# Two mixture-of-experts layers: one-hots by narrow comparisons, gathers issued one tile earlier, weights loaded between stores

## The chip, the cores and the metric

One core of a Trainium2 chip runs the whole network in one launch. The metric is the device time of that launch in microseconds (us). Three runs of the kernel before gave 2677.88, 2682.55 and 2683.99 us, so the median is 2682.55 us. "us" is always microseconds and "ns" nanoseconds.

## The reference, cut to what matters

The network has eight stages on x of shape (8, 512, 256), that is 4096 tokens of 256 numbers: attention, mixture, attention, a feed-forward layer, a windowed attention, mixture, attention, a feed-forward layer. Each stage is `x = x + stage(layernorm(x))`. The change touches only the two mixtures, called L0 and L2 here:

```
z = layernorm(x)
logits = z @ gate                       # 8 experts
take the two largest, weights = softmax over the two
L0 expert e:  h = z @ w1[e] + b1[e]     # 256 -> 512
              h = gelu(layernorm(h) * g[e] + b[e])
              y = h @ w2[e] + b2[e]     # 512 -> 256
              out = layernorm(sum of weight * y, plus z) * ln_g + ln_b
L2 expert e:  h = gelu(z @ w1[e] + b1[e])   # 256 -> 1024
              y = h @ w2[e] + b2[e]         # 1024 -> 256
              out = sum of weight * y
x = x + out
```

## The kernel before, in words

x stays in the on-chip memory, 128 tokens to a tile, 32 tiles of 256 columns, in 8 batches of 4 tiles. Everything is float32 unless said otherwise. A mixture has three parts that follow one another, with a barrier between them.

**Dispatch** (`dispatch`, lines 793 to 1051) finds which expert each token goes to. ScalarE normalises a batch (`normalise`, line 917), SyncE stores it to the rows_in table in device memory (line 856), and TensorE turns it (line 873) and multiplies it by the gate (line 881). In L0 there is a buffer for each of the 8 batches. In L2 there are two, so `normalise(b)` waits until the store of batch b - 2 has landed. After the first store SyncE issues `k.late(sp)` and the expert constants. In L2 `k.late` issues eight loads of 1 MB, one expert's first layer each, all in a row, and the stores of the other seven batches come behind them on the same queue. In L0 `k.late` does nothing, since those weights came earlier.

VectorE then picks the two experts of each token (`select`, lines 965 to 976, once for each half of the tokens) and works out each row's place in a table of 71 tiles of 128 rows, each owned by one expert. To turn places into lists of row numbers it goes through 8 chunks of 8 columns (lines 1030 to 1036). A chunk needs two sets of 0/1 vectors in bf16: `at_tile`, 8 x 71, made by one VectorE comparison (line 1033), and `at_slot`, 8 x 128, made by another (line 1035: 1024 float32 elements against a broadcast column). `at_tile` is multiplied by two kinds of constants, by ScalarE (line 938) and by GpSimd (line 947), and TensorE multiplies the result by `at_slot` (line 904). The end of this is `src` and `dst`, 71 columns of row numbers, and `owner`, the expert of each tile.

**Experts** (L0: `experts`, lines 1082 to 1263; L2: `experts_gelu`). The 71 tiles run one after the other. In L0, step j of each engine is:

- TensorE: transpose h of tile j (line 1154), first layer of tile j + 2 (line 1145), transpose the rows of tile j + 3 (`turn`, line 1136), second layer of tile j (line 1164).
- ScalarE: gelu of tile j (line 1187), then the copy of the transposed rows of tile j + 3 (line 1179).
- VectorE: add b1 to tile j + 2 and take its mean and variance (lines 1207 to 1213), then add b2 to the output of tile j (line 1227), then centre h of tile j + 2 (line 1217).
- GpSimd: send the output of tile j - 1 to the rows_out table (`send_rows`, line 1277, an indirect DMA that waits for line 1227), fetch the rows of tile j + 3 (`fetch_rows`, line 1269, an indirect DMA that waits until the buffer's former rows are transposed), take the inverse root of the variance of tile j + 2 (line 1242), and in each odd step up to 31 add the bias `ln_b` to two tiles of x (`bias`, line 1246).

Gathered rows have two buffers, used in turn. An engine runs its own list in order, so a wait also holds whatever comes behind it. TensorE, ScalarE and VectorE read the owner of a tile into a register in each step (`value_load`).

**Combine** (L0: `combine_norm`) reads the rows back, weighs, adds and normalises them. It is not changed.

Of the kernel before, what the change touches and what calls it, by code (L numbers as in the profile page):

```python
# [16 lines left out]
BF16 = mybir.dt.bfloat16  # L17
# [776 lines left out]
def dispatch(nc, k, L):  # L794
# [12 lines left out]
    with ctx:  # L807
        gate = sb(nm + "gate", [P, DC, E])
        shift = sb(nm + "shift", [P, NT])
        Z = NB if L == 0 else 2  # L810
# [19 lines left out]
        code = sb(nm + "code", [P, NT])  # L830
        top = [sb(f"{nm}top{j}", [P, NT]) for j in range(TOPK)]
# [18 lines left out]
        with nc.Block() as block:  # L850
            @block.sync
            def _(sp):
                sp.dma_start(gate[:, :, :], k.a[f"L{L}_gate"]).then_inc(w_in, 16)
                for b in range(NB):
                    sp.wait_ge(z_done, b + 1)
                    sp.dma_start(k.zs[P + b * SEQ:P + (b + 1) * SEQ, :].rearrange("(t p) d -> p t d", p=P),
                                 z[b % Z].rearrange("p (t d) -> p t d", t=TPB)).then_inc(stored[b % 2], 16)
                    if b == 0:
                        k.late(sp)
                        load_expert_constants(sp, k, L)  # L860
                for s in range(2):
                    sp.wait_ge(stored[s], 16 * NB // 2)
                sp.wait_ge(k.zeroed, 16)
# [77 lines left out]
            @block.gpsimd  # L941
            def _(pool):
                for c in range(CHUNKS):
                    s = c % 2
                    pool.wait_ge(hot_done, c + 1)
                    hi = k.cst[:, C_HI + c * NJ:C_HI + (c + 1) * NJ, None].to_broadcast([P, NJ, NTILES])
                    pool.tensor_tensor(names[s][:, :, 0, :], at_tile[s][:, :, :], hi, ALU.mult).then_inc(hi_done, 1)

            @block.vector
            def _(dve):  # L950
# [29 lines left out]
                dve.sem_inc(centred, 1)  # L980
                for h in range(2):
# [48 lines left out]
                for c in range(CHUNKS):  # L1030
# [4 lines left out]
                    dve.tensor_tensor(at_slot[s][:, :, :], k.cst[:, None, C_I:C_I + P].to_broadcast([P, NJ, P]),  # L1035
                                      slot[:, own, None].to_broadcast([P, NJ, P]), ALU.is_equal).then_inc(slot_done, 1)
# [45 lines left out]
def experts(nc, k, L):  # L1082
# [15 lines left out]
    with ctx:  # L1098
        w1, w2 = k.w1, k.w2
        b2, bt, b1, gt, post_b = k.expert_constants  # L1100
        if norm:
            st = [sb(f"{nm}st{s}", [P, 6]) for s in range(2)]
# [21 lines left out]
        with nc.Block() as block:  # L1124
# [114 lines left out]
            def _(pool):  # L1239
# [4 lines left out]
                def bias(i):  # L1244
                    xs = k.x[:, i * (2 * D):(i + 1) * (2 * D)].rearrange("p (t d) -> p t d", t=2)
                    pool.tensor_tensor(xs, xs, post_b[:, None, :].to_broadcast([P, 2, D]), ALU.add)
# [289 lines left out]
def load_expert_constants(eng, k, L):  # L1536
    for t, (name, spread) in zip(k.expert_constants, (("b2", True), ("bt", False), ("b1", True), ("gt", False),
                                                      ("ln_b", True))[:5 if L == 0 else 2]):
# [5 lines left out]
def mixture(nc, k, L):  # L1544

    ctx, sb, ps, sem = scoped(k)
    with ctx:
# [4 lines left out]
            [sb("x0_b1", [P, E * F]), sb("x0_gt", [P, E * FC]), sb("x0_post_b", [P, D])] if L == 0 else [None] * 3)  # L1552
# [806 lines left out]
def build(nc, a, out, stages="a0 m0 a1 f1 w2 m2 a3 f3"):  # L2359
    nothing = lambda sp: None  # L2360
    with ExitStack() as ctx:
# [35 lines left out]
        if "m0" in todo:  # L2397
            k.w1, k.w2 = room("m0_w1", E * DC * F0), room("m0_w2", E * F0 // P * D)
            k.w_count = 16 * 2 * E
            k.late = m0_weights if first_stage("m0") else nothing  # L2400
# [28 lines left out]
        if "m2" in todo:  # L2429
            k.w1 = room("m2_w1", E * DC * F2)  # L2430

            def m2_late(eng):
                if "a1" not in todo:
                    load_second_layers(eng, k, 2)
                load_first_layers(eng, k, 2, range(E))
# [67 lines left out]
```

## Time and profile before

| | |
|---|---|
| median of three runs | 2682.55 us |
| the profiled execution, whole | 2691.29 us |
| its span | 2689.5 us |
| TensorE busy (matmul) | 2075.9 us, 77% |
| TensorE busy (weight load, overlapping) | 1525.3 us, 57% |
| VectorE busy | 1327.2 us, 49% |
| ScalarE busy | 936.7 us, 35% |
| GpSimd busy | 598.0 us, 22% |
| mean granted TensorE clock | 0.877 of full |

The span is one execution from its first to its last instruction. The profile names engines PE (TensorE matmul), PEld (TensorE weight load), DVE (VectorE), ACT (ScalarE), POOL (GpSimd) and SP (SyncE, SPq for what its queue issues). The page's own split of the span into 40 slices shows L0's mixture in slices 4 to 15 and L2's in slices 25 to 34. The busy share is a mean over stages with different limits, so each stage has to be read by itself.

### The profile page before, as it was taken

The numbers are of one execution on the slowest core, as the hardware profiler recorded it, in microseconds if no ns is written. First come the engines' busy times: TensorE is split into PE (matmuls) and PEld (weight loads), VectorE is DVE, ScalarE is ACT, GpSimd is POOL, SyncE is SP. The second block draws the span as 40 slices with busy tenths as digits, with TensorE's granted clock in tenths as the row PEclk, the third lists the DMA queues.
The fourth block names the chain that finished last, engine by engine and source line by source line (L and its number), as shares of the span: only waits on it lengthen the run. The fifth ranks groups of instructions, "written<-read, shape, count | busy, mean of one in ns | idle before, by whom it ended". The sixth has DMA issues, their size and how long they took to land. (4 is left out here: it accounts for less than half of the span.)

```text
span 2689.5 us, 37832 instructions
## 1 busy us (share of the span) xinstructions
PE 2075.9 (77%) x11915; PEld 1525.3 (57%) x11931; DVE 1327.2 (49%) x2988; ACT 936.7 (35%) x2034; POOL 598.0 (22%) x580
## 2 busy tenths in 40 slices
PE   6997466666666611997999795579999999699687
PEld 4666243443443310665566663579999999366355
DVE  5873522222222257676777562422222222588787
ACT  3444221112112132443333122323333333355487
POOL 1210433332222255012011000122222222122000
PEclk9996688888878865998999896579999999799799
DMA  6003100000000032200000003111111111410000
GB/s 227 1 1 113 36 29 29 27 27 27 29 28 28 27 119 78 105 1 1 12 0 0 6 10 145 59 44 38 36 35 37 37 35 32 137 48 1 1 32 32
DMA packets 66898, 115.34 MB, mean 43 GB/s; under 512 B 13520, under 2 KB 50512, under 8 KB 63728
## 3 DMA queue, kind: packets, MB, share of 16 engines
q1 hardware_dynamic: 51536, 74.56, 8.0%
q0 software_dynamic: 13680, 37.37, 4.4%
q10 hardware_dynamic: 1584, 2.13, 0.3%
q8 instruction: 58, 0.95, 0.2%
q14 instruction: 40, 0.33, 0.0%
HBM read 82.71 MB, written 31.33 MB: 42 GB/s over the span
## 5 line engine op out<-in xcount | busy, mean ns | idle before, releaser
L1336 PEld LDWEIGHTS psum<-e_xT,e_w 128*128 128x128 f32 x2272 | 269.7, 195 | 8.4 <-ACT e_xT L1366 4.9
L1336 PE MATMUL psum<-e_xT,e_w 128*128 128x128 f32 x2272 | 270.3, 278 | 4.2 <-ACT e_xT L1366 4.2
L1373 ACT ACTIVATE e_hT<-psum,x_bt 128x128 f32<-128x128 f32 x568 | 154.6, 383 | 337.3 <-PE psum L1336 323.4
L268 POOL TENSOR_TENSOR rstd<-lnt,half 128x4 f32<-128x4 f32 (+1 forms) x72 | 81.0, 1126 | 820.0 <-DVE lnt L262 820.0
L1345 PE MATMUL psum<-m_w,e_hT 128*128 x1136 | 256.8, 379 | 0.0
L1164 PE MATMUL psum<-m_w,e_hT 128*128 x568 | 215.9, 547 | 39.7 <-issue 36.1
L1345 PEld LDWEIGHTS psum<-m_w,e_hT 128*128 128x128 f32 x1136 | 210.4, 190 | 25.7
L1277 POOL DMA_INDIRECT rows_out<-e_y,dst x106 | 111.1, 1048 | 512.0 <-DVE e_y L1227 337.0
L1394 DVE COPY e_w<-m_w 128x2048 f32 x71 | 87.1, 1227 | 239.0 <-PE psum L1336 228.5
L1227 DVE TENSOR_TENSOR e_y<-psum,x_b 128x256 f32<-128x256 f32 x71 | 30.2, 425 | 353.2 <-PE psum L1164 352.6
L1187 ACT ACTIVATE e_hT<-psum,x_bt,x_gt 128x128 f32<-128x128 f32 x284 | 107.0, 457 | 275.2 <-PE psum L1154 275.2
L1164 PEld LDWEIGHTS psum<-m_w,e_hT 128*128 128x128 f32 x568 | 146.4, 269 | 85.0 <-issue 57.5
L1136 PE MATMUL psum<-cst,e_x 128*128 128x128 f32 x142 | 32.8, 315 | 197.9 <-DMA e_x<-rows_in,src 197.9
L696 DVE TENSOR_REDUCE a_mx<-psum 128x8 f32<-128x512 f32 x192 | 123.2, 684 | 106.8 <-PE psum L500 106.5
L1136 PEld LDWEIGHTS psum<-cst,e_x 128*128 128x128 f32 x142 | 15.1, 147 | 256.1 <-DMA e_x<-rows_in,src 245.9
L1269 POOL DMA_INDIRECT e_x<-rows_in,src x142 | 139.2, 980 | 63.5 <-issue 42.0
L625 ACT ACTIVATE a_pT<-psum 128x512 f32<-128x512 f32 x192 | 104.0, 593 | 126.8 <-PE psum L550 126.8
L1145 PE MATMUL psum<-m_w,e_xT 128*128 x284 | 144.4, 633 | 1.4 <-ACT e_xT L1179 1.2
L1806 PE MATMUL psum<-f_w,f_q 128*128 128x256 f32 x512 | 123.9, 388 | 14.7 <-DVE f_q L1693 14.7
L481 PE MATMUL psum<-a_cx,att_wk 128*128 128x64 f32 x192 | 29.9, 305 | 130.4 <-DMA a_cx<-in_ctxT 130.4
L1806 PEld LDWEIGHTS psum<-f_w,f_q 128*128 128x128 f32 x512 | 98.9, 194 | 55.5 <-issue 30.5
L699 DVE TENSOR_TENSOR a_pr<-psum,a_mx 128x512 f32<-128x512 f32 x192 | 122.9, 682 | 0.7
(285 smaller groups left out, 3935.0 us busy)
## 6 DMA issues: line engine op xcount, KB each, us to landing
m_w<-in_L_ffn_w SPq DMA_DIRECT2D x16, 1024.0 KB, 15.2
m_w<-in_L_ffn_w SPq DMA_DIRECT2D x16, 512.0 KB, 12.2
c_g<-rows_out SPq DMA_DIRECT2D x16, 512.0 KB, 5.0
a_ar_g<-rows_out SPq DMA_DIRECT2D x16, 512.0 KB, 5.1
x_res<-in_x SPq DMA_DIRECT2D x8, 512.0 KB, 7.1
rows_in<-x_z SPq DMA_DIRECT2D x8, 512.0 KB, 7.4
rows_in<-r_work SPq DMA_DIRECT2D x8, 512.0 KB, 3.3
out_x<-x_res SPq DMA_DIRECT2D x8, 512.0 KB, 2.9
```

Of the source, the lines that this page charges most:

```text
L625: act.activation(pT[t // 2][:, g * SLOTS:(g + 1) * SLOTS, t % 2, :], tr_b[g][:, :, :], ACT.Exp).then_inc(t_evac, 1)
L696: dve.tensor_reduce(mx[g][:, :], wide[g], AX.X, ALU.max).then_inc(s_max, 1)
L699: dve.tensor_tensor(pr[t % 2][:, g * W:(g + 1) * W].rearrange("p (h l) -> p h l", h=HPC), wide[g], mx[g][:, :, None].to_broadcast([P, HPC, ...
L1145: mm = pe.matmul(h_b[s][:, c * 512:(c + 1) * 512], xT[s][:, kk, :], w1[:, bass.ds(e * (DC * F) + (kk * F + c * 512), 512)], start=(kk == 0 ...
L1164: mm = pe.matmul(y_b[:, 0:D], hT[s][:, f, :], w2[:, bass.ds(e * (FC * D) + f * D, D)], start=(f == 0), stop=(f == FC - 1))
L1187: g = act.activation(hT[s][:, f, :], hT_b[:, f, :], ACT.Gelu, bias=bt[:, col], scale=gt[:, col] if norm else 1.0)
L1269: pool.indirect_dma_start(out=xin[j % 2][:, :], out_offset=None, in_=k.zs[:, :], in_offset=bass.IndirectOffsetOnAxis(ap=k.src[:, j:j + 1], ...
L1277: pool.indirect_dma_start(out=k.ys[:, :], out_offset=bass.IndirectOffsetOnAxis(ap=k.dst[:, j:j + 1], axis=0), in_=y[j % 2][:, :], in_offse ...
L1336: mm = pe.matmul(h_b[s][:, f, :], w1[:, kk, f * P:(f + 1) * P], xT[s][:, kk, :], start=(kk == 0), stop=(kk == DC - 1))
L1345: mm = pe.matmul(y_b[s][:, 0:D], hT[s][:, f, :], k.w2[:, bass.ds(e * (FC * D) + f * D, D)], start=(f == 0), stop=(f == FC - 1))
L1373: g = act.activation(hT[s][:, f, :], h_b[s][:, f, :], ACT.Gelu, bias=bt[:, bass.ds(e * FC + f, 1)])
L1806: mm = pe.matmul(yb[t % 2][:, 0:D], q[s][:, g, t * P:(t + 1) * P], w2[:, g, :], start=(g == 0), stop=(g == FC - 1))
```

## The change

1. In the dispatch of both mixtures `at_slot` is made by 8 VectorE comparisons of 128 bf16 elements with one float32 column each (`tensor_scalar`), in place of one comparison of 1024 float32 elements with a broadcast. There are 64 of them in a dispatch in place of 8. The numbers 0 to 127 are copied once to bf16 (`numbers`).
2. In the experts of L0, GpSimd fetches the rows of tile j + 4 ahead of sending tile j - 1, in place of tile j + 3 behind it. One more fetch is issued before the loop.
3. The bias `ln_b` of L0 is added to x by GpSimd in the dispatch, in 8 additions of 1024 columns, each when its batch has been normalised, and no longer in the experts, where it took 16 of 512 columns. It has its own buffer and semaphore now, and its load is issued ahead of the stores.
4. In the dispatch of L2 the expert constants are issued after the first store as before, but the eight loads of 1 MB are spread: one behind each of the stores 1 to 6, two behind store 7.

```diff
@@ dispatch, tiles
+        if L == 0:
+            post_b, post_in = sb(nm + "post_b", [P, D]), sem(nm + "post_in")
+        numbers = sb(nm + "numbers", [P, P], BF16)
@@ dispatch, SyncE
                 sp.dma_start(gate[:, :, :], k.a[f"L{L}_gate"]).then_inc(w_in, 16)
+                if L == 0:
+                    sp.dma_start(post_b[:, :], k.a["L0_ffn_ln_b"].partition_broadcast(P)).then_inc(post_in, 16)
                 for b in range(NB):
                     sp.wait_ge(z_done, b + 1)
                     sp.dma_start(k.zs[P + b * SEQ:P + (b + 1) * SEQ, :].rearrange("(t p) d -> p t d", p=P),
                                  z[b % Z].rearrange("p (t d) -> p t d", t=TPB)).then_inc(stored[b % 2], 16)
                     if b == 0:
-                        k.late(sp)
                         load_expert_constants(sp, k, L)
+                    k.late(sp, b)
@@ dispatch, GpSimd
+                if L == 0:
+                    pool.wait_ge(post_in, 16)
+                    for b in range(NB):
+                        pool.wait_ge(z_done, b + 1)
+                        xs = k.x[:, b * (TPB * D):(b + 1) * (TPB * D)].rearrange("p (t d) -> p t d", t=TPB)
+                        pool.tensor_tensor(xs, xs, post_b[:, None, :].to_broadcast([P, TPB, D]), ALU.add)
@@ dispatch, VectorE
+                then(dve.tensor_copy(numbers[:, :], k.cst[:, C_I:C_I + P]))
...
-                    dve.tensor_tensor(at_slot[s][:, :, :], k.cst[:, None, C_I:C_I + P].to_broadcast([P, NJ, P]),
-                                      slot[:, own, None].to_broadcast([P, NJ, P]), ALU.is_equal).then_inc(slot_done, 1)
+                    for i in range(NJ):
+                        nj = c * NJ + i
+                        o = dve.tensor_scalar(at_slot[s][:, i, :], numbers[:, :], slot[:, nj:nj + 1], None, ALU.is_equal)
+                    o.then_inc(slot_done, 1)
@@ experts, GpSimd (A is 2 in L0)
                 for j in range(A + 1):
                     fetch_rows(pool, k, j, xin, xT_ps)
-                pool.wait_ge(k.const_in, k.consts)
                 for j in range(A):
                     root(j)
+                fetch_rows(pool, k, A + 1, xin, xT_ps)
                 for j in range(NTILES):
+                    if j + A + 2 < NTILES:
+                        fetch_rows(pool, k, j + A + 2, xin, xT_ps)
                     if j > 0:
                         send_rows(pool, k, j - 1, y, y_done)
-                    if j + A + 1 < NTILES:
-                        fetch_rows(pool, k, j + A + 1, xin, xT_ps)
                     if j + A < NTILES:
                         root(j + A)
-                    if j % 2 and j // 2 < NT // 2:
-                        bias(j // 2)
@@ the loads of L2
-            def m2_late(eng):
+            def m2_late(eng, b):
...
-                load_first_layers(eng, k, 2, range(E))
+                if b > 0:
+                    load_first_layers(eng, k, 2, (b - 1,))
+                if b == NB - 1:
+                    load_first_layers(eng, k, 2, range(b, E))
```

## Rows read from the trace of the kernel before

**Rows 1.** Engine busy times by window: PE, PEld, DVE, ACT, POOL, clock, DMA, GB/s
```profile
600.00:700.00 100.00, 62.27 (x199) 39.01 (x198) 28.63 (x67) 20.79 (x55) 29.64 (x34) 0.88 0.09 28
1860.00:1960.00 100.00, 100.00 (x689) 94.22 (x689) 23.13 (x28) 34.33 (x126) 26.49 (x27) 1.00 0.11 35
...
1660.00:1686.00 26.00, 4.82 (x38) 4.72 (x38) 0.00 (x0) 2.28 (x5) 0.00 (x0) 0.57 0.96 383
```

**Rows 2.** Waits in L0's experts (298 to 962 us): total, times, longest
```profile
PE psum L1136 <- DMA e_x<-rows_in,src: 197.9, 69, 8.3
```

**Rows 3.** Timeline of one step of L0's experts: start, length, engine, line, operation
```profile
502.68 0.42 DVE L1227 TENSOR_TENSOR e_y<-psum,x_b 128x256 f32<-128x256 f32 x1 [5.63 <-PE psum L1164]
...
503.40 1.08 POOL L1277 DMA_INDIRECT rows_out<-e_y,dst  x1 [5.70 <-DVE e_y L1227]
...
504.78 0.97 POOL L1269 DMA_INDIRECT e_x<-rows_in,src  x1 [0.30 <-issue]
...
507.55 0.44 PE L1136 MATMUL psum<-cst,e_x 128*128 128x128 f32 x2 [2.68 <-DMA e_x<-rows_in,src]
```

**Rows 4.** Line 1227, all its instructions: ns min/median/max, first and last start
```profile
L1227 DVE TENSOR_TENSOR e_y<-psum,x_b x71: 424/425/426, 321.6 to 958.1; 128x256 f32<-128x256 f32 x71
```

**Rows 5.** Timeline of TensorE alone, a warm step, then the prologue
```profile
603.40 1.99 PE L1164 MATMUL psum<-m_w,e_hT 128*128 x8 [0.55 <-issue]
605.23 0.60 PE L1154 MATMUL psum<-cst,e_h 128*128 128x128 f32 x4
605.66 1.90 PE L1145 MATMUL psum<-m_w,e_xT 128*128 x4
...
309.11 1.98 PE L1145 MATMUL psum<-m_w,e_xT 128*128 x4 [0.56 <-ACT e_xT L1179]
...
310.92 0.38 PE L1136 MATMUL psum<-cst,e_x 128*128 128x128 f32 x2
```

**Rows 6.** Timeline of L0's last steps, where no rows are gathered
```profile
940.86 3.77 PE L1164 MATMUL psum<-m_w,e_hT 128*128 x8 [0.30 <-issue]
...
947.97 0.69 DVE L1207 TENSOR_TENSOR e_h<-psum,x_b 128x512 f32<-128x512 f32 x1 [2.21 <-PE psum L1145]
...
950.53 0.42 DVE L1227 TENSOR_TENSOR e_y<-psum,x_b 128x256 f32<-128x256 f32 x1 [0.69 <-issue]
950.87 0.54 DVE L1217 TENSOR_SCALAR e_h<-e_h,e_mv,e_rs 128x512 f32<-128x512 f32 x1
...
953.61 0.60 PE L1154 MATMUL psum<-cst,e_h 128*128 128x128 f32 x4
...
956.00 1.99 PE L1164 MATMUL psum<-m_w,e_hT 128*128 x8 [1.80 <-ACT e_hT L1187]
```

**Rows 7.** Timeline of L2's dispatch, then of L0's: ScalarE
```profile
1685.77 2.07 ACT L917 ACTIVATE r_work<-x_res,r_shift,rstd 128x256 f32<-128x256 f32 x4 [23.72 <-DMA rows_in<-r_work]
...
235.01 1.02 ACT L924 ACTIVATE r_work<-psum 128x1024 f32<-128x1024 f32 x1 [2.03 <-PE psum L873]
```

**Rows 8.** Timeline of a chunk of L0's dispatch
```profile
272.39 1.22 DVE L1035 TENSOR_TENSOR att_wq<-cst,r_slot 128x1024 bf16<-128x1024 f32 x1
...
272.55 2.05 POOL L947 TENSOR_TENSOR r_work<-r_work,cst 128x568 bf16<-128x568 bf16 x1 [56.90 <-DVE r_work L1033]
273.52 1.68 DVE L1033 TENSOR_TENSOR r_work<-cst,r_tile 128x568 bf16<-128x568 f32 x1
...
275.12 1.21 DVE L1035 TENSOR_TENSOR att_wk<-cst,r_slot 128x1024 bf16<-128x1024 f32 x1
```

**Rows 9.** Timeline: small VectorE operations with a scalar
```profile
205.22 0.16 DVE L259 TENSOR_SCALAR mean<-mean 128x4 f32<-128x4 f32 x1
205.29 0.16 DVE L260 TENSOR_SCALAR lnt<-lnt 128x4 f32<-128x4 f32 x1
...
267.45 0.20 DVE L1010 TENSOR_SCALAR r_turn<-r_rank 128x64 f32<-128x64 f32 x1
```

**Rows 10.** Groups of instructions of the whole run: GpSimd
```profile
L436 POOL TENSOR_TENSOR x_res<-x_res,att_bo 128x1024 f32<-128x1024 f32 x24 | 56.8, 2365 | 8.6 <-ACT a_z L589 8.6
```

More of the change, by code:

```diff
@@ L1099, in experts @@
         w1, w2 = k.w1, k.w2
-        b2, bt, b1, gt, post_b = k.expert_constants
+        b2, bt = k.expert_constants[0:2]
         if norm:
+            b1, gt = k.expert_constants[2:4]
             st = [sb(f"{nm}st{s}", [P, 6]) for s in range(2)]
@@ L1242, in root @@
                     pool.tensor_tensor(rs[j % 2][:, :], ve[j % 2][:, :], k.half[:, 0:1], ALU.pow).then_inc(rsq, 1)
-                def bias(i):
-                    xs = k.x[:, i * (2 * D):(i + 1) * (2 * D)].rearrange("p (t d) -> p t d", t=2)
-                    pool.tensor_tensor(xs, xs, post_b[:, None, :].to_broadcast([P, 2, D]), ALU.add)
                 for j in range(A + 1):
                     fetch_rows(pool, k, j, xin, xT_ps)
-                pool.wait_ge(k.const_in, k.consts)
                 for j in range(A):
                     root(j)
+                fetch_rows(pool, k, A + 1, xin, xT_ps)
                 for j in range(NTILES):
+                    if j + A + 2 < NTILES:
+                        fetch_rows(pool, k, j + A + 2, xin, xT_ps)
                     if j > 0:
                         send_rows(pool, k, j - 1, y, y_done)
-                    if j + A + 1 < NTILES:
-                        fetch_rows(pool, k, j + A + 1, xin, xT_ps)
                     if j + A < NTILES:
                         root(j + A)
-                    if j % 2 and j // 2 < NT // 2:
-                        bias(j // 2)
                 send_rows(pool, k, NTILES - 1, y, y_done)
@@ L1536, in load_expert_constants @@
 def load_expert_constants(eng, k, L):
-    for t, (name, spread) in zip(k.expert_constants, (("b2", True), ("bt", False), ("b1", True), ("gt", False),
-                                                      ("ln_b", True))[:5 if L == 0 else 2]):
+    for t, (name, spread) in zip(k.expert_constants, (("b2", True), ("bt", False), ("b1", True), ("gt", False)
+                                                      )[:4 if L == 0 else 2]):
         src = k.a[f"L{L}_ffn_{name}"]
@@ L1551, in mixture @@
         k.expert_constants = [sb(f"x{L}_b2", [P, E * D]), sb(f"x{L}_bt", [P, E * FC])] + (
-            [sb("x0_b1", [P, E * F]), sb("x0_gt", [P, E * FC]), sb("x0_post_b", [P, D])] if L == 0 else [None] * 3)
+            [sb("x0_b1", [P, E * F]), sb("x0_gt", [P, E * FC])] if L == 0 else [])
         if L == 0:
@@ L2399, in build @@
             k.w_count = 16 * 2 * E
-            k.late = m0_weights if first_stage("m0") else nothing
+            k.late = (lambda eng, b: m0_weights(eng) if b == 0 else None) if first_stage("m0") else lambda eng, b: None
         if "a0" in todo:
@@ L2430, in build @@
             k.w1 = room("m2_w1", E * DC * F2)
-            def m2_late(eng):
-                if "a1" not in todo:
+            def m2_late(eng, b):
+                if b == 0 and "a1" not in todo:
                     load_second_layers(eng, k, 2)
-                load_first_layers(eng, k, 2, range(E))
+                if b > 0:
+                    load_first_layers(eng, k, 2, (b - 1,))
+                if b == NB - 1:
+                    load_first_layers(eng, k, 2, range(b, E))
             k.late = m2_late
```

## The prediction

> **What bounds the kernel now.** I read the busy times by window first, then the waits of the stage that stands out, then its timeline step by step, and at the end the two dispatches side by side.
>
> The windows show two expert stages that look alike in code and not in time [rows 1]. In L2's experts TensorE is busy 100.00 us of 100, at full clock. In L0's it is busy 62.27 us of 100 and no other engine passes 30, so nothing is saturated there: something late is waited for. The waits name it [rows 2]: TensorE's transpose (L1136) sits idle 197.9 us in 69 waits for gathered rows, 2.9 us a tile.
>
> The timeline shows why the rows are late [rows 3]. The output of a tile starts at 502.68; GpSimd sends it from 503.40 on; only then, at 504.78, does it issue the gather, because in its list the gather stands behind the send; the rows are used at 507.55. The second layer comes behind that transpose in TensorE's list, so the next output waits for it, and so the next send and the next gather. Output, send, gather, transpose, second layer is a closed loop, 4.87 us of it (502.68 to 507.55) outside TensorE. Line 1227 runs 71 times from 321.6 to 958.1 [rows 4]: 70 steps in 636.5 us, 9.09 us each.
>
> The dispatches have one clear stall [rows 7]: ScalarE waits 23.72 us in L2 for a store of the second batch that stands behind eight 1 MB loads. L0 runs the same code with more buffers and without those loads.
>
> **Part 1, gathers a tile further ahead (the large term).** GpSimd now issues gather j + 4 before it waits for output j - 1. The gather waits for its buffer alone, which is free once rows j + 2 are transposed, a step and more before. From issue to use it takes 2.77 us (504.78 to 507.55) [rows 3] and it now has nearly two steps. So the loop is cut and the wait of [rows 2] goes. What is queued behind the gather's wait on GpSimd is send j - 1 and root j + 2; the transpose waited for stands ahead of the second layer that the send waits for, so this wait is over first. GpSimd's own work in a step is the gather 0.97, the send 1.08, a root and gaps: under 4 us.
>
> What is late next? TensorE itself. A warm step is the second layer 1.83 us (start to start, 603.40 to 605.23), the transposes of h 0.43 (605.23 to 605.66), the first layer 1.81 (309.11 to 310.92) and the transpose of rows 0.38 [rows 5]: 4.45 us. Two other chains must stay below it:
> - gelu: from the transposes of h to the second layer that waits for gelu it takes 2.39 us (953.61 to 956.00) [rows 6], and 1.83 for the second layer follow: 4.22 us.
> - VectorE: 2.56 us from L1207 to L1227 (947.97 to 950.53), 0.34 to L1217, 0.54 for it, and at most 0.69 to the next [rows 6]: 4.13 us.
>
> Both are below 4.45 but close, so there is no further slack. The step could be as short as 4.22 (the transposes overlap more than their length says). It could be 5.00, if the 0.55 us between the transpose of rows and the second layer stays [rows 5]. That gap is a register load behind a wait; with the wait gone TensorE's sequencer can run ahead and hide it. I take 4.45, clock at full level (2.4 GHz): L2's experts hold 1.00 at 100% busy, where L0's have 0.88 with holes in them [rows 1].
>
> 70 steps x (9.09 - 4.45) = **325 us** saved. Bounds: 70 x (9.09 - 4.22) = 341, and 70 x (9.09 - 5.00) = 286.
>
> **Part 2, loads between the stores of L2.** The 23.72 us stall goes [rows 7]. What takes its place: each store now stands behind at most one load of 1 MB (the second store behind the 1 MB of constants). At 383 GB/s [rows 1] a load is 2.7 us and a store of 0.5 MB 1.4, together 4.1 a batch. A batch of L0 takes ScalarE 1.02 + 2.07 us of work and 2.03 of waiting for TensorE [rows 7], 5.1 in all, so the queue just keeps up. With two buffers I allow 2 us for the first batches: **22 us** saved. Bounds 17 (a us lost in each later batch) and 24. Two loads are left behind the last store, 5.5 us at that rate, while the eight chunks alone last four times as long; the experts find them landed. SyncE has nothing else to do there.
>
> **Part 3, the bias moved.** 8 additions of 2.37 us [rows 10], 19 us on GpSimd, which had been idle 56.90 us when the first chunk came [rows 8]; they follow the batches. They end long before the chunks, whose products are the next thing in GpSimd's list. They can hold up `select` of the first half of the tokens, which is early anyway. In the experts GpSimd was waiting, not working, so taking the bias out saves nothing there. Its 128 KB load ahead of the first store costs under 1 us, and L0's stores have buffers of their own. If the cover were gone in full it would cost 19 us. I take **0**.
>
> **Part 4, narrow comparisons.** The wide comparison holds VectorE 1.13 us (272.39 to 273.52) [rows 8]. A chunk takes 2.73 us (272.39 to 275.12), and the three operations lie end to end: GpSimd's product spans 2.05 but the comparison at 273.52 ends, at 275.20, 0.60 us after the product's end at 274.60, where its own elements at about 1 ns each need 0.59. I read this as turns: VectorE's comparison, GpSimd's product (about 1 us of its 2.05), VectorE's next. So a chunk changes by what VectorE's part changes by. The trace has no 128-column bf16 comparison with a column. Nearest rows [rows 9]: two tiny scalar operations start 0.07 us apart (205.22, 205.29), and one of 64 float32 columns is 0.20 long with its pipeline. I take 0.10 each, nearer the start-to-start figure, since no wait stands between the eight: 0.80 against 1.13, 0.33 x 16 chunks = **5 us** saved. Ends: at 0.20 each a loss of 0.47 x 16 = 7.5 us; at 0.07 a gain of 9, and 15 more if GpSimd's product no longer takes its turn. The copy of the numbers to bf16 falls where VectorE waits for logits: 0.
>
> One rule speaks against this part. The Trainium skill, "VectorE: DVE Perf Modes", in the section on the TRN2 errata, says that the memory latency is paid between instructions, so one large operation pays it once and many small ones each time, and advises 512 elements or more. Its cycle formula there (58 plus the elements over 4, at 0.96 GHz) would give, as an estimate, 94 ns for each of the eight, 0.75 us together; its section "The DRAIN you can't avoid" says that the next operation can't issue until the pipeline is empty. By the first the sum would be as mine within 1 us; by the second it would be near the losing end. The 0.07 us between two starts speaks against the second [rows 9].
>
> **The sum.** Own time 2691.3 - 325 - 22 - 0 - 5 = 2339 us. The profiled execution is 8.7 us above the median of the three runs, so against the median: **2331 us**, 13% less.
>
> **The rivals.**
> - The comparisons are held one behind the other, 0.20 us each with the whole length paid: +7.5 in place of -5, 2343 us. For it: the small operations last 0.16 to 0.20. Against: their starts lie closer. It moves the sum, not the verdict. Chance 0.20.
> - The register loads stay in TensorE's (or VectorE's) step: 5.00 us a step, 39 us more, 2370 us. For it: 0.55 us of idle is there even in warm steps [rows 5], and 0.69 us before L1227 where its input was ready [rows 6]. Against: in both places a wait had just held the sequencer. Chance 0.13.
> - TensorE stays at its lower level (1.2 GHz) in L0's experts: the second layer lasts 3.77 us there against 1.99 [rows 5, 6]; a step of 2 x 4.45 = 8.9 us saves 13, giving 2642 us. For it: the clock is below full today. Against: L2's experts [rows 1]. Chance 0.05.
> - The change does not do what it says: the gather still lands late (held in GpSimd's list by something I took as early), and the gains of the dispatch are eaten by port conflicts with the moved bias. About 2683 us. Against: each wait ahead of the gather belongs to the step before. Chance 0.02.
> - Slower: denser matmuls bring the granted clock down, and it stays down after L0's experts. The place is L2's experts, about 520 us at full clock with TensorE always busy; at the lower level they last 520 us more. With all other gains as above it decides from two thirds of that stage (350 of 520); in full, 2850 us. For it: only that the clock varies today. Against: in L2's experts it is 1.00 through hundreds of us at 100% busy [rows 1]. Chance 0.03.
>
> **How the numbers follow.** The likeliest case has 0.57, and its own range is 2305 to 2355 (step 4.22 to 4.7). Low end of the whole range: 2683 - 341 - 24 - 18 = 2300. High end: the 5.00 us step (2370) with the comparisons at 0.20 (+12), the worse dispatch (+5) and some cold steps: 2395. Left out are the last three cases, 0.10, and a little at both ends. A difference under 0.2% (5 us; the three runs spread 6) can't be told from none. Faster: 0.57 + 0.20 + 0.13 + 0.05 = 0.95; same 0.02; slower 0.03.
>
> **What would show it.** In L0's experts: L1136 no longer waits for rows; L1227 runs 71 times in about 312 us in place of 636; TensorE over 90% busy with a granted clock near 1.00. If its step is 5 us, idle of "issue" stands before L1164. GpSimd's gather stands about 4 us or more before its use. In L2's dispatch no ScalarE wait over 3 us for a store. A chunk of 2.4 us in place of 2.73; 3.2 means held comparisons. My prediction is wrong if the step is over 5.1 us, which would mean a chain that I have not seen (the gelu's, or VectorE's, longer than I read), or if the clock does not rise.

## The result

The changed kernel takes 2327.36 us (median of 4 runs, 2324.47 to 2330.43), the kernel before 2680.22 us in the same session. The ratio is 0.8685, 95% interval 0.8663 to 0.8706: 13% faster. The forecast was 2331 us. The profiled execution of the changed kernel takes 2330.43 us, its span is 2328.6 us, 360.9 us shorter than that of before. The medians lie 352.9 us apart: the profiled execution of the kernel before was a long one.

Where the 360.9 us of span went. The marks are the starts of single instructions in the two traces: a dispatch runs from its load of the gate (L853, now L856) to its last VectorE operation (L1051, now L1065):

| stretch | before | changed | difference |
|---|---|---|---|
| start to L0's dispatch | 216.6 | 217.5 | +0.9 |
| dispatch of L0 | 80.1 | 81.5 | +1.4 |
| experts of L0, to the last addition of b2 (L1227, now L1242) | 661.4 | 322.8 | -338.6 |
| from there to L2's dispatch | 695.2 | 691.7 | -3.5 |
| dispatch of L2 | 103.3 | 84.2 | -19.1 |
| rest | 932.9 | 930.9 | -2.0 |

**L0's experts, after.** Busy time by window, columns as in [rows 1]:

```profile
400.00:500.00 100.00, 100.00 (x429) 68.37 (x429) 61.74 (x143) 44.23 (x118) 60.67 (x72) 1.00 0.20 63
299.00:620.00 321.00, 306.28 (x1272) 205.68 (x1273) 184.68 (x426) 135.51 (x356) 181.95 (x212) 0.97 0.20 62
```

Past its first tiles TensorE is busy without a hole and at its full clock level, where [rows 1] had 62 us of 100 and 0.88; over the whole stage it is 306 us of 321 and 0.97. Next, all instructions of the line that adds b2 (L1227 before, L1242 now; compare [rows 4]), and what is left of TensorE's waits in the stage (total, times, longest; compare [rows 2]):

```profile
L1242 DVE TENSOR_TENSOR e_y<-psum,x_b x71: 423/425/427, 325.1 to 621.8; 128x256 f32<-128x256 f32 x71
```

```profile
PE psum L1151 <- DMA e_x<-rows_in,src: 11.3, 2, 8.5
...
PE psum L1179 <- ACT e_hT L1202: 3.6, 2, 1.8
```

71 additions start within 296.7 us, so a step is 4.24 us; before it was 9.09. Of 69 waits for rows 2 are left, the first rows of the stage and one more. The timeline of one step (start, length) answers to [rows 3 and 5]:

```profile
452.39 0.60 PE L1169 MATMUL psum<-cst,e_h 128*128 128x128 f32 x4
...
452.83 1.88 PE L1160 MATMUL psum<-m_w,e_xT 128*128 x4
...
453.43 1.01 POOL L1278 DMA_INDIRECT e_x<-rows_in,src  x1 [0.19 <-issue]
453.44 0.42 DVE L1242 TENSOR_TENSOR e_y<-psum,x_b 128x256 f32<-128x256 f32 x1 [0.85 <-PE psum L1179]
...
454.55 0.38 PE L1151 MATMUL psum<-cst,e_x 128*128 128x128 f32 x2
...
454.74 1.01 POOL L1286 DMA_INDIRECT rows_out<-e_y,dst  x1 [0.30 <-issue]
...
454.79 1.99 PE L1179 MATMUL psum<-m_w,e_hT 128*128 x8
...
456.62 0.60 PE L1169 MATMUL psum<-cst,e_h 128*128 128x128 f32 x4
```

The gather at 453.43 is issued at the same moment as an output is made (453.44), and no longer behind the send of that output (454.74). Nothing of TensorE's waits for it. The 0.55 us of "issue" between L1151 and L1179 is gone: the second layer starts 0.24 us after L1151 (454.55 to 454.79). From L1169 to L1169 it is 4.23 us.

**The chunks, after** (L0's dispatch; compare [rows 8]), and all narrow comparisons of one buffer with ns min/median/max:

```profile
276.17 2.33 DVE L1049 TENSOR_SCALAR att_wk<-r_numbers,r_slot 128x128 bf16<-128x128 bf16 x8
...
276.33 1.16 POOL L958 TENSOR_TENSOR r_work<-r_work,cst 128x568 bf16<-128x568 bf16 x1 [1.76 <-DVE r_work L1045]
278.42 0.73 DVE L1045 TENSOR_TENSOR r_work<-cst,r_tile 128x568 bf16<-128x568 f32 x1
...
279.08 2.33 DVE L1049 TENSOR_SCALAR att_wq<-r_numbers,r_slot 128x128 bf16<-128x128 bf16 x8
```

```profile
L1049 DVE TENSOR_SCALAR att_wq<-r_numbers,r_slot x64: 237/241/1199, 273.3 to 1391.5; 128x128 bf16<-128x128 bf16 x64
```

A chunk now takes 2.91 us (276.17 to 279.08), 2.73 before. GpSimd's product is down from 2.05 to 1.16 us and `at_tile` from 1.68 to 0.73, but the eight comparisons last 2.33 where the wide one lasted 1.21. Seven of the eight last about 0.24 us and start 0.16 apart. One, beside GpSimd's product, lasts about 1.19 us (the 1199 is its longest): GpSimd's turn now falls among the narrow comparisons and no longer on `at_tile`.

**L2's dispatch, after** (compare [rows 7]):

```profile
1319.34 2.07 ACT L922 ACTIVATE r_work<-x_res,r_shift,rstd 128x256 f32<-128x256 f32 x4 [0.35 <-DMA rows_in<-r_work]
...
1325.40 2.07 ACT L922 ACTIVATE r_work<-x_res,r_shift,rstd 128x256 f32<-128x256 f32 x4 [3.08 <-DMA rows_in<-r_work]
...
1327.53 1.97 PE L878 MATMUL psum<-cst,r_work 128*128 128x128 f32 x8 [2.25 <-ACT r_work L922]
...
1329.14 2.07 ACT L922 ACTIVATE r_work<-x_res,r_shift,rstd 128x256 f32<-128x256 f32 x4 [0.76 <-DMA rows_in<-r_work]
```

The 23.72 us wait is gone. A 3.08 us wait for the third store has come, and TensorE (L878) waits 2.25 us for what follows it. The 3.08 us are just over the 3 us that the prediction set as the most such a wait should be. The next four waits are of 0.76 to 0.91 us, and from 1327.53 on TensorE (L878, L886) is idle before none of its work on the batches.

**The bias, after:** it runs in L0's dispatch as was said. It holds up two operations of the first `select`: one run of L985, below, lasts 2.38 us and one of L982 lasts 1.62, where each took 0.29 before. The second `select` starts after 11.17 us of waiting for TensorE, so these 3.4 us cost nothing.

```profile
243.98 2.35 POOL L953 TENSOR_TENSOR x_res<-x_res,r_post_b 128x1024 f32<-128x1024 f32 x1 [2.67 <-ACT x_z L922]
244.10 2.38 DVE L985 TENSOR_TENSOR att_wv<-r_eq,r_code 128x128 f32<-128x128 f32 x1
```

### The profile page after: what moved, and what is told of

The parts are those of the page before. It is cut to its first block and busy times, and to the rows that moved or that the text cites. A ratio compares the mean times of both kernels' runs of the same rounds, so it can differ in the third digit from the quotient of the medians.

```text
span 2328.6 us, 37955 instructions
## 1 busy us (share of the span) xinstructions
PE 1958.2 (84%) x11930; PEld 1464.6 (63%) x11931; DVE 1333.6 (57%) x3102; ACT 937.1 (40%) x2034; POOL 579.6 (25%) x572
## 5 line engine op out<-in xcount | busy, mean ns | idle before, releaser
L1354 PE MATMUL psum<-m_w,e_hT 128*128 x1136 | 256.8, 379 | 0.0
L1354 PEld LDWEIGHTS psum<-m_w,e_hT 128*128 128x128 f32 x1136 | 210.4, 190 | 25.7
L1403 DVE COPY e_w<-m_w 128x2048 f32 x71 | 87.1, 1227 | 226.6 <-PE psum L1345 225.2
L1286 POOL DMA_INDIRECT rows_out<-e_y,dst x106 | 105.9, 999 | 206.1 <-DVE e_y L1413 175.0
L1179 PE MATMUL psum<-m_w,e_hT 128*128 x568 | 140.6, 391 | 4.0 <-ACT e_hT L1202 3.6
L1160 PE MATMUL psum<-m_w,e_xT 128*128 x284 | 139.7, 615 | 1.2 <-ACT e_xT L1194 1.2
L1802 PE MATMUL psum<-f_zT,f_w 128*128 128x512 f32 x256 | 121.9, 602 | 0.9 <-DVE f_q L1699 0.9
L1179 PEld LDWEIGHTS psum<-m_w,e_hT 128*128 128x128 f32 x568 | 102.5, 190 | 21.2 <-issue 5.5
L481 PEld LDWEIGHTS psum<-a_cx,att_wk 128*128 128x128 f32 x192 | 26.5, 214 | 136.7 <-issue 136.7
L472 PE MATMUL psum<-a_zT,att_wq 128*128 128x512 f32 x192 | 104.0, 668 | 7.3 <-ACT a_qT L602 5.2
```

Source lines behind the costliest of these rows:

```text
L1160: mm = pe.matmul(h_b[s][:, c * 512:(c + 1) * 512], xT[s][:, kk, :], w1[:, bass.ds(e * (DC * F) + (kk * F + c * 512), 512)], start=(kk == 0 ...
L1179: mm = pe.matmul(y_b[:, 0:D], hT[s][:, f, :], w2[:, bass.ds(e * (FC * D) + f * D, D)], start=(f == 0), stop=(f == FC - 1))
L1286: pool.indirect_dma_start(out=k.ys[:, :], out_offset=bass.IndirectOffsetOnAxis(ap=k.dst[:, j:j + 1], axis=0), in_=y[j % 2][:, :], in_offse ...
L1354: mm = pe.matmul(y_b[s][:, 0:D], hT[s][:, f, :], k.w2[:, bass.ds(e * (FC * D) + f * D, D)], start=(f == 0), stop=(f == FC - 1))
L1802: mm = pe.matmul(hb[f % HS][:, :], w1[:, kk, f * P:(f + 1) * P], zT[s][:, kk, :], start=(kk == 0), stop=(kk == DC - 1))
```

## The experiments

In each group the kernels ran on one chip, next to the kernel before. "Changed" is the kernel after the change.

### What cuts the loop: e1, e2, e3

**e1, the gathers alone** (bias, loads and comparisons as before):

```diff
@@ experts, GpSimd, in the kernel before
                 for j in range(A):
                     root(j)
+                fetch_rows(pool, k, A + 1, xin, xT_ps)
                 for j in range(NTILES):
+                    if j + A + 2 < NTILES:
+                        fetch_rows(pool, k, j + A + 2, xin, xT_ps)
                     if j > 0:
                         send_rows(pool, k, j - 1, y, y_done)
-                    if j + A + 1 < NTILES:
-                        fetch_rows(pool, k, j + A + 1, xin, xT_ps)
```

> The kernel before with the experts' gathers alone changed (issued ahead of the send and one tile further ahead); the bias stays in the experts. Theory (TensorE's own work is the new bound): L1227's 71 runs span 297 us as in the changed kernel (636.5 before), whole run about 2340 us, 340 less than before. Rival (moving the bias mattered too): GpSimd has 0.97 + 1.05 + 0.57 us and gaps of 0.3 each, some 3.5 us a step, and 1.25 more in each odd step of the first 32; that is 4.7 in those against 4.24, so the first 32 steps become longer by up to 0.5 us every other step and the whole by 5 to 15 us: 2345 to 2355.

Measured: 2343.45 us, ratio 0.8736 (0.8685 to 0.8787). The additions of b2, and the busy times of a window in which the bias still runs:

```profile
L1227 DVE TENSOR_TENSOR e_y<-psum,x_b x71: 424/425/426, 322.3 to 618.6; 128x256 f32<-128x256 f32 x71
```

```profile
340.00:440.00 100.00, 100.00 (x425) 67.89 (x424) 67.67 (x142) 45.28 (x120) 75.73 (x84) 1.00 0.19 61
```

296.3 us for the 71, the same as in the changed kernel. GpSimd is busy 75.73 of 100 us with the bias in its list, and TensorE still has no hole. So the gathers bring all of the 340 us, and the bias cost nothing where it was. The rival, which wanted the stage 5 to 15 us longer, is out. The whole agrees: 2683.51 us, the kernel before in this group, less 340 is 2343.5.

**e2, one tile further ahead but behind the send:**

```diff
@@ experts, GpSimd, in the changed kernel
                 for j in range(NTILES):
-                    if j + A + 2 < NTILES:
-                        fetch_rows(pool, k, j + A + 2, xin, xT_ps)
                     if j > 0:
                         send_rows(pool, k, j - 1, y, y_done)
+                    if j + A + 2 < NTILES:
+                        fetch_rows(pool, k, j + A + 2, xin, xT_ps)
```

> The changed kernel, but the gather of tile j + 4 stands behind the send of tile j - 1, as in the kernel before; only the distance is kept. Theory A (the distance of one tile is what cuts the loop): the rows then land 4.9 us after the output of tile j - 1 starts, and are needed one step and 2.3 us later, so nothing waits: 4.24 us a step, 297 us, as in the changed kernel. Theory B (the order is what cuts it): the wait for rows comes back, some 2 us a step or more, 400 us or longer for the 71 tiles.

Measured: 2337.92 us (one run).

```profile
L1242 DVE TENSOR_TENSOR e_y<-psum,x_b x71: 424/425/426, 324.2 to 630.5; 128x256 f32<-128x256 f32 x71
```

306.3 us, 4.38 a step: theory A in the main, but it expected 297 and no wait at all. The 9.6 us more than in the changed kernel show in TensorE's waits (the loads of weights, PEld, come ahead of the matmuls that use them):

```profile
PEld psum L1151 <- DMA e_x<-rows_in,src: 14.6, 32, 3.7
```

The changed kernel has 1 such wait in place of 32. In the changed kernel the second layer follows the start of the transpose of rows by 0.22 to 0.25 us in 67 of 68 steps; here by more than 0.3 in 37 of 68, and what is over 0.24 adds up to 9.6 us. Behind the send, the gather lands only just in time.

**e3, ahead of the send but no tile further:**

```diff
@@ experts, GpSimd, in the changed kernel
-                fetch_rows(pool, k, A + 1, xin, xT_ps)
                 for j in range(NTILES):
-                    if j + A + 2 < NTILES:
-                        fetch_rows(pool, k, j + A + 2, xin, xT_ps)
+                    if j + A + 1 < NTILES:
+                        fetch_rows(pool, k, j + A + 1, xin, xT_ps)
```

> The changed kernel, but the gather is that of tile j + 3 again, issued ahead of the send; only the order is kept. Theory A (distance): a second loop remains, first layer, VectorE's statistics 1.9 us, GpSimd's root 0.8, gather 0.3 + 2.8 to landing, transpose, which is one step round; about 5.9 us a step, 410 us for the 71 tiles, 115 us more than the changed kernel (about 2440). Theory B (order): 4.24 us a step as in the changed kernel.

Measured: 2433.48 us (one run). All additions of b2, then the timeline:

```profile
L1242 DVE TENSOR_TENSOR e_y<-psum,x_b x71: 424/425/426, 327.1 to 726.2; 128x256 f32<-128x256 f32 x71
```

```profile
450.10 0.44 PE L1151 MATMUL psum<-cst,e_x 128*128 128x128 f32 x2 [1.51 <-DMA e_x<-rows_in,src]
...
451.18 1.99 PE L1179 MATMUL psum<-m_w,e_hT 128*128 x8 [0.64 <-issue]
...
455.17 0.38 PE L1151 MATMUL psum<-cst,e_x 128*128 128x128 f32 x2
...
455.41 1.99 PE L1179 MATMUL psum<-m_w,e_hT 128*128 x8
...
457.19 0.15 DVE L1228 TENSOR_SCALAR e_ve<-e_mv 128x1 f32<-128x1 f32 x1
...
457.43 0.56 POOL L1257 TENSOR_TENSOR e_rs<-e_ve,half 128x1 f32<-128x1 f32 x1 [2.26 <-DVE e_ve L1228]
...
458.18 1.01 POOL L1277 DMA_INDIRECT e_x<-rows_in,src  x1 [0.19 <-issue]
...
460.97 0.44 PE L1151 MATMUL psum<-cst,e_x 128*128 128x128 f32 x2 [1.40 <-DMA e_x<-rows_in,src]
```

399.1 us, 5.70 a step, against 5.9 expected. The timeline shows the second loop: statistics (L1228), root (L1257), gather (458.18), transpose 2.79 us later (460.97), with a wait for rows in every other step. It also shows the 0.55 us of "issue" of [rows 5] come and go: behind a transpose that had to wait (450.10) TensorE is idle for 0.64 us before the second layer, behind one that had not (455.17) the second layer starts 0.24 us later.

So of the 340 us the distance alone brings 330, the order alone 237. The order takes the send out of the loop of [rows 3]. The distance leaves it in, but gives one time round the loop a step more. With both, the gather has no output ahead of it and a step of slack.

### What bounds the step now: e4

The edit leaves out the second half of each sum of L0's first layer, so two of its four matrix products of a tile:

```diff
@@ experts, TensorE, layer1
-                        for kk in range(DC):
+                        for kk in range(1):
                             mm = pe.matmul(h_b[s][:, c * 512:(c + 1) * 512], xT[s][:, kk, :],
...
-                                           start=(kk == 0), stop=(kk == DC - 1))
+                                           start=True, stop=True)
```

> The changed kernel with half of L0's first layer left out (two of its four matrix products of each tile), so 0.9 us less work for TensorE a step. If TensorE alone sets the step of 4.24 us, it falls to about 3.35 (235 us for the 71 tiles). If the chain of the gelu is as long (2.40 us from the transposes of h to the second layer, then 1.83), as the rows of before had it (4.22), the step stays at about 4.2 and TensorE gets idle time of 0.9 us in front of the second layer.

Measured: 2325.75 us (one run).

```profile
L1242 DVE TENSOR_TENSOR e_y<-psum,x_b x71: 424/425/426, 321.4 to 617.4; 128x256 f32<-128x256 f32 x71
```

```profile
454.75 1.99 PE L1179 MATMUL psum<-m_w,e_hT 128*128 x8 [0.72 <-ACT e_hT L1202]
...
456.58 0.60 PE L1169 MATMUL psum<-cst,e_h 128*128 128x128 f32 x4
...
458.98 1.99 PE L1179 MATMUL psum<-m_w,e_hT 128*128 x8 [0.72 <-ACT e_hT L1202]
```

296.0 us for the 71: with 0.9 us less work for TensorE a step, the step is the same. TensorE waits 0.72 us for the gelu in front of each second layer, and from L1169 (456.58) to L1179 (458.98) it is 2.40 us, as the tail of the kernel before had it [rows 6]. In the changed kernel the same stretch is 2.40 us (452.39 to 454.79) without a wait, 0.44 + 1.72 + 0.24 of TensorE's own work. So TensorE's work and the chain of the gelu are equally long. A lighter TensorE alone brings nothing here; both would have to be shortened. The reverse, a shorter gelu alone, was not tried.

### The other three parts, each alone: e5, e6, e7

**e5, the loads alone** (the fourth item of the change on the kernel before):

```diff
@@ dispatch, SyncE, in the kernel before
                     if b == 0:
-                        k.late(sp)
                         load_expert_constants(sp, k, L)
+                    k.late(sp, b)
```

> The kernel before with the loads of L2's first layers spread between the stores, and nothing else. Theory: ScalarE's 23.7 us wait goes and a 3 us wait for the third store comes, so the dispatch of L2 is 18 to 21 us shorter and so is the whole: about 2661 us. Rival (the loads then take bandwidth from something later, or the time comes back in the experts): under 12 us gained.

Measured: 2659.69 us, ratio 0.9921 (0.9900 to 0.9942). L2's dispatch takes 82.6 us in place of 103.3, 20.7 less, and 20.1 us show in the whole. The stretch varies a little by itself: in e1 and e7, whose loads are those of before, it takes 101.4 and 101.2, so the gain is 18.6 to 20.7 us. The longest wait left:

```profile
1658.78 2.07 ACT L917 ACTIVATE r_work<-x_res,r_shift,rstd 128x256 f32<-128x256 f32 x4 [3.01 <-DMA rows_in<-r_work]
```

**e6, the narrow comparisons alone** (the first item on the kernel before):

```diff
@@ dispatch, VectorE, in the kernel before
-                    dve.tensor_tensor(at_slot[s][:, :, :], k.cst[:, None, C_I:C_I + P].to_broadcast([P, NJ, P]),
-                                      slot[:, own, None].to_broadcast([P, NJ, P]), ALU.is_equal).then_inc(slot_done, 1)
+                    for i in range(NJ):
+                        nj = c * NJ + i
+                        o = dve.tensor_scalar(at_slot[s][:, i, :], numbers[:, :], slot[:, nj:nj + 1], None, ALU.is_equal)
+                    o.then_inc(slot_done, 1)
```

> The kernel before with the narrow bf16 comparisons alone. Theory (turns on a shared port, 0.16 us from one narrow comparison to the next): a chunk takes 2.9 us against 2.73, each dispatch is 1.4 us longer, the whole 3 us longer (ratio 1.001). Rival (my sum before the result, 0.10 us each): a chunk of 2.4 us, 5 us shorter (ratio 0.998).

Measured: 2685.27 us against 2679.80, ratio 1.0025 (1.0005 to 1.0045).

```profile
277.10 2.33 DVE L1039 TENSOR_SCALAR att_wk<-r_numbers,r_slot 128x128 bf16<-128x128 bf16 x8
279.35 0.74 DVE L1035 TENSOR_TENSOR r_work<-cst,r_tile 128x568 bf16<-128x568 f32 x1
280.01 2.17 DVE L1039 TENSOR_SCALAR att_wq<-r_numbers,r_slot 128x128 bf16<-128x128 bf16 x7
```

A chunk of 2.91 us again, and from the first `at_tile` to the end of the dispatch 26.4 us in place of 25.0. The two dispatches account for 3 us, the whole is 5.5 us longer; what the rest may be is in the last section. Slower is clear of the interval; my first sum is out.

**e7, the bias alone** (third item, `ln_b` added in the dispatch):

```diff
@@ experts, GpSimd, in the kernel before
-                    if j % 2 and j // 2 < NT // 2:
-                        bias(j // 2)
@@ dispatch, GpSimd
+                if L == 0:
+                    pool.wait_ge(post_in, 16)
+                    for b in range(NB):
+                        pool.wait_ge(z_done, b + 1)
...
+                        pool.tensor_tensor(xs, xs, post_b[:, None, :].to_broadcast([P, TPB, D]), ALU.add)
```

> The kernel before with the bias moved into the dispatch, and nothing else. Theory: no change, within 1 us in each stage (GpSimd idle in both places; the half of the tokens that is selected first is delayed by 2 to 4 us and is not waited for). Rival (the products of the dispatch or the stores are delayed): the dispatch of L0 2 to 10 us longer.

Measured: 2676.48 us, ratio 0.9991 (0.9969 to 1.0013): no difference. L0's dispatch takes 80.2 us in place of 80.1. In the experts "within 1 us" can't be told: the 71 additions take 629.4 us here and 636.5 in the kernel before, but 630.6 in e5 and 632.5 in e6, which have the experts of before unchanged.

### Why the narrow comparisons lose, and a better chunk: e8 to e12

**e8, narrow comparisons of float32 numbers** (the copy of the numbers to bf16 goes too):

```diff
@@ dispatch, VectorE, in the changed kernel
-                        o = dve.tensor_scalar(at_slot[s][:, i, :], numbers[:, :], slot[:, nj:nj + 1], None, ALU.is_equal)
+                        o = dve.tensor_scalar(at_slot[s][:, i, :], k.cst[:, C_I:C_I + P], slot[:, nj:nj + 1], None, ALU.is_equal)
```

> The changed kernel with the 64 narrow comparisons reading the float32 numbers instead of the bf16 copy (result still bf16). If a fixed cost rules (0.16 us from start to start whatever the type), the chunk stays at 2.91 us. If the elements rule (128 float32 at half the rate of bf16, 0.03 to 0.07 us more each), the chunk takes 3.15 to 3.5 us.

Measured: 2332.12 us (one run); a chunk of 3.13 us (277.27 to 280.40).

```profile
277.27 2.55 DVE L1048 TENSOR_SCALAR att_wq<-cst,r_slot 128x128 bf16<-128x128 f32 x8
...
280.40 2.55 DVE L1048 TENSOR_SCALAR att_wk<-cst,r_slot 128x128 bf16<-128x128 f32 x8
```

A cost that is fixed whatever the type is out. The chunk is 0.02 us under the low end of the second expectation: the type is worth 0.22 us a chunk, 0.03 a comparison. If the bf16 elements go at twice the rate of float32, as that expectation supposed, they take some 0.03 of the 0.16 us (an estimate), and the rest is fixed.

**e9, the changed kernel again,** on the chip of the next three.

> The changed kernel as it is, on the same chip as the three below, so that they can be compared with it: 0.8685 of before, about 2327 us.

Measured: 2330.19 us (2328.75 to 2331.39, 5 runs), ratio 0.8699 (0.8678 to 0.8721).

**e10, the changed kernel with the wide comparison:** the edit of e6 taken back in the changed kernel.

```diff
@@ dispatch, VectorE, in the changed kernel
-                    for i in range(NJ):
...
+                    dve.tensor_tensor(at_slot[s][:, :, :], k.cst[:, None, C_I:C_I + P].to_broadcast([P, NJ, P]),
+                                      slot[:, own, None].to_broadcast([P, NJ, P]), ALU.is_equal).then_inc(slot_done, 1)
```

> The changed kernel with the wide comparison of before in both dispatches (part 4 undone). Theory (turns, narrow ones dearer): chunk 2.73 us in place of 2.91, 3 us less in the whole than the changed kernel. Rival (part 4 is a gain through something outside the chunks): 3 us or more longer than the changed kernel.

Measured: 2323.40 us (2320.28 to 2327.13, 5 runs), ratio 0.8676 (0.8654 to 0.8699).

```profile
276.58 1.21 DVE L1045 TENSOR_TENSOR att_wq<-cst,r_slot 128x1024 bf16<-128x1024 f32 x1
...
276.74 2.05 POOL L957 TENSOR_TENSOR r_work<-r_work,cst 128x568 bf16<-128x568 bf16 x1 [0.68 <-DVE r_work L1043]
277.72 1.67 DVE L1043 TENSOR_TENSOR r_work<-cst,r_tile 128x568 bf16<-128x568 f32 x1
...
279.31 1.21 DVE L1045 TENSOR_TENSOR att_wk<-cst,r_slot 128x1024 bf16<-128x1024 f32 x1
```

The chunk is back at 2.73 us, and from the first `at_tile` to the end each dispatch is 1.4 us shorter (25.0 in place of 26.4). That is the 3 us expected. The rest of the 6.8 us between the medians is not explained: behind L2's dispatch, which the edit does not touch, the profiled execution of e10 is also 3.2 us shorter than that of e9.

**e11, the same, and GpSimd's product made by VectorE:**

```diff
@@ dispatch, in the last kernel: the loop of GpSimd goes, VectorE gets
+                    dve.wait_ge(hot_done, c + 1)
+                    hi = k.cst[:, C_HI + c * NJ:C_HI + (c + 1) * NJ, None].to_broadcast([P, NJ, NTILES])
+                    dve.tensor_tensor(names[s][:, :, 0, :], at_tile[s][:, :, :], hi, ALU.mult).then_inc(hi_done, 1)
```

> As the one with the wide comparison, and the product of GpSimd in each chunk is made by VectorE. Theory (VectorE and GpSimd take turns, so GpSimd's 0.95 us lie in the chunk and a product on VectorE takes 0.66 in their place): chunk of 0.66 + 1.13 + 0.66 = 2.45 us against 2.73, 4.5 us less in the whole. Rival (they run beside each other and VectorE waits for nothing but its own pace): VectorE gets 0.66 us more, chunk 3.4 us, 10 us more in the whole.

Measured: 2321.60 us (2319.94 to 2326.35, 5 runs), ratio 0.8671 (0.8648 to 0.8693).

```profile
278.37 1.22 DVE L1040 TENSOR_TENSOR att_wk<-cst,r_slot 128x1024 bf16<-128x1024 f32 x1
279.51 0.75 DVE L1044 TENSOR_TENSOR r_work<-r_work,cst 128x568 bf16<-128x568 bf16 x1
280.17 0.74 DVE L1038 TENSOR_TENSOR r_work<-cst,r_tile 128x568 bf16<-128x568 f32 x1
280.83 1.22 DVE L1040 TENSOR_TENSOR att_wq<-cst,r_slot 128x1024 bf16<-128x1024 f32 x1
```

VectorE has one operation more in each chunk and the chunk is shorter: 2.46 us (278.37 to 280.83). `at_tile` takes 0.74 where it took 1.67 beside GpSimd. The same stretch of each dispatch takes 22.8 us in place of 25.0, together 4.4 of the 4.5 us expected. In the whole only 1.8 us show, within the spread of the runs.

**e12, the same, and all loads of L2's dispatch behind the last store:**

```diff
@@ dispatch, SyncE
-                    if b == 0:
+                    if b == (0 if L == 0 else NB - 1):
                         load_expert_constants(sp, k, L)
                     k.late(sp, b)
@@ the loads of L2
-                if b > 0:
-                    load_first_layers(eng, k, 2, (b - 1,))
                 if b == NB - 1:
-                    load_first_layers(eng, k, 2, range(b, E))
+                    load_first_layers(eng, k, 2, range(E))
```

> As the last, and in L2's dispatch all eight loads and the expert constants are issued behind the last store. Theory (the 3 us wait for the third store is contention with the loads; after the last store there are over 50 us in which the queue is empty and 9 MB need 25): dispatch of L2 at the pace of L0's, 3 to 4 us less than the last; experts of L2 start as before. Together some 10 us less than the changed kernel, about 2317 us. Rival: the loads land too late and the first tile of L2's experts waits for them: 5 to 10 us more than the last.

Measured: 2317.49 us (2314.52 to 2321.97, 5 runs), ratio 0.8651 (0.8627 to 0.8674). The longest wait for a store is now:

```profile
1313.05 2.07 ACT L921 ACTIVATE r_work<-x_res,r_shift,rstd 128x256 f32<-128x256 f32 x4 [0.53 <-DMA rows_in<-r_work]
```

L2's dispatch takes 77.9 us, exactly as L0's, 2.5 less than in e11. Its experts start as before: TensorE's first work there waits for gathered rows and not for weights, and comes 6.7 us behind the last operation of the dispatch, in e11 6.8. Against the changed kernel on the same chip (e9) it is 12.7 us or 0.5% less, and the runs of the two do not overlap. It beats both kernels.

## Why the prediction was right

The predicted time came out 3.6 us from the measured one. The large term and its mechanism were right. That the total is so close is in part luck: the step's term was 9 to 15 us too small, the comparisons' 8 too large and the loads' up to 3 too large, and these errors cancel.

- **The closed loop, and the wait that goes.** As predicted; e1 shows that this part alone brings all of it. The prediction did not part distance from order; e2 and e3 show that either alone brings most of it, and the distance more (330 and 237 us of 340).
- **What is late next.** The step was put at 4.45 us, bounds 4.22 and 5.00; it is 4.24, so the term was 340 us and not 325. Against the stage as e5 and e6 have it (630.6 and 632.5 us in place of 636.5) it was 334 to 336. The mis-sized pieces are the transpose of rows, taken at its length of 0.38 us [rows 5] where it takes 0.24 from start to start, and the first layer, 1.81 in the prologue and 1.72 now (452.83 to 454.55). The chain of the gelu, 4.22, was within 0.02 of the step. e4 shows that it binds as hard as TensorE, where the prediction called TensorE alone late next.
- **The register loads.** The rival of 5.00 us a step is out: without a wait in front, the 0.55 us vanish, and in e3 they come back in just those steps whose transpose waits. That it is the register load that fills them was argued from the kernel's text, not tested by itself.
- **The clock.** It rose to 1.00 in the windows without holes. The rival of a low clock is out, and so is the slower one: the stretch with L2's experts is 2.0 us shorter than before.
- **The loads.** 22 us predicted, bounds 17 and 24. The dispatch is 18.6 to 20.7 us shorter by e5; in the changed kernel 19.1, after the comparisons took 1.4 back. Where 2 us were allowed for the first batches, a wait of 3.08 us stands.
- **The bias.** 0 predicted, and none found in e1 and e7. It does hold up `select` of the first half, as the prediction said, and nothing waits for it.
- **The comparisons.** This step failed in sign: a gain of 5 us was predicted, 3 us were lost (1.4 in each dispatch). The turns held. VectorE and GpSimd take turns: e11 removes GpSimd's turn and the chunk shrinks by 0.27 us although VectorE has more to do. The narrow comparison was mis-sized: 0.10 us from start to start was taken, 0.16 is measured, so eight take 1.28 where the wide one takes 1.13, and a chunk of 0.66 + 1.28 and some 0.97 for GpSimd's turn is the 2.91 measured. The row I leaned on, 0.07 us between two starts [rows 9], is of 4 elements; the one of 64 float32 elements, 0.20, was the other end, and the truth lies nearer to that. The low end of the whole range took 18 us for this part, which neither of its own ends gives (9, or 24 with GpSimd's turn gone).

By the Trainium skill, "VectorE: DVE Perf Modes", section on the TRN2 errata, small operations pay a fixed latency each; the trace agrees in direction, since 8 of 128 cost more than one of 1024. The formula there gives, as an estimate, 94 ns, and the measured 0.16 us decides against it. The same page's section "The DRAIN you can't avoid" says that the next operation does not start until the pipeline is empty, and adds that one that is not held starts earlier. The trace shows the second: a comparison lasts 0.24 us (median 241 ns), and the next starts 0.16 us after its start.

On the turns: `at_tile` lasts 1.67 us beside GpSimd's product and 0.74 alone (e11). The Trainium skill, "SBUF — State Buffer", section "Who interferes with whom", says that a VectorE operation with two inputs in the on-chip memory and a GpSimd operation that reads there exclude one another; the trace agrees.

## What to carry to other kernels

When an engine is idle for data that another engine fetches, look at what stands ahead of the fetch in that engine's own list. If it is something that waits for a result of the same step, the transfer's latency is in a loop, and issuing it one tile earlier gives it the time of a whole step, even if its place in the list stays (330 of 340 us here); moving it ahead as well took out the rest. Before you expect the new step to equal the busiest engine's work, add up the next chain from start to start; here the gelu's was within 0.02 us of it. One wide operation against many narrow ones is decided by the start-to-start time of the narrow one, so take that from a row of like size, not from the smallest.

## What was not expected of the hardware

The first 55 us of L0's dispatch, in which no edit changed TensorE's work, take either 55.1 or 58.3 us in the 14 profiled executions, and nothing in between. The gate products of the first batch tell them apart: 1.91 us in the kernel before, 3.42 in e6. Behind each row stands the granted clock of the same moment (columns as in [rows 1]).

```profile
222.86 1.91 PE L881 MATMUL psum<-r_gate,r_work 128*128 128x8 f32 x16
```

```profile
223.00:225.00 2.00, 2.00 (x21) 2.00 (x20) 0.00 (x0) 2.00 (x5) 0.00 (x0) 1.00 1.01 314
```

```profile
221.55 3.42 PE L882 MATMUL psum<-r_gate,r_work 128*128 128x8 f32 x16
```

```profile
223.00:225.00 2.00, 2.00 (x11) 2.00 (x11) 0.00 (x0) 2.00 (x4) 0.00 (x0) 0.50 1.09 426
```

These are the two clock levels of TensorE (2.4 and 1.2 GHz). In both cases TensorE had just run sixteen transposes behind a wait of 6.33 us. In the fast case the higher level lasts for the first two batches only. From the third on the gate products take 3.42 us in both, at 0.50, although TensorE is busy for 9.00 us of 9.00 (231 to 240 us). In L2's experts [rows 1] it was busy for 100.00 of 100 at 1.00. e1, e5, e6 and e8 had the slow case in their profiled runs, the others the fast one, with no relation to the edit that I can see. So 3 us of difference in one execution can come from this place alone, and it may be part of the 5.5 us of e6. What decides it was not tried.
